# Differential attention: the six middle turns of the loop over batches written out on all five engines

## The reference, cut to what matters

```
x = x + layernorm(differential_attention(layernorm(x)))      # the stage of this case
x = x + layernorm(windowed_attention_and_gated_ffn(layernorm(x)))   # two layers
x = x + layernorm(diffusion_attention(layernorm(x)))
x = x + layernorm(expert_mixture(layernorm(x)))

# differential attention, for each batch and head, causal:
attn = softmax(Q1 K1^T / 4) - lam * softmax(Q2 K2^T / 4)
O = attn V;  O = O / rms(O) * rms_scale * 0.2;  out = concat(O) Wo^T
```

## Time and profile before

| | |
|---|---|
| median of 3 runs | 4381.61 us |
| the profiled execution's own time | 4382.84 us |
| its span, first to last instruction | 4381.0 us |
| the changed stage, up to the barrier | 1188 us |
| PE busy over the whole span | 3709.8 us (85%) |
| DVE, ACT, POOL busy | 2415.1, 1752.6, 1619.3 us |
| granted TensorE clock, mean | 0.924 |

### The profile page before, as it was taken

The page is one execution under the profiler, slowest core; times in us unless marked ns, Lnnn a source line. Parts: engine busy times, 40 slices in busy tenths (PEclk is TensorE's granted clock), DMA queues, the critical chain, the costliest instruction groups (busy, mean ns, idle before and its releaser), DMA issues. The chain is left out here.

```text
span 4381.0 us, 64166 instructions
## 1 busy us (share of the span) xinstructions
PE 3709.8 (85%) x17520; PEld 2209.8 (50%) x17584; DVE 2415.1 (55%) x6529; ACT 1752.6 (40%) x4010; POOL 1619.3 (37%) x1750
## 2 busy tenths in 40 slices
PE   6999999999689998997999899679999998459940
PEld 3555555566345555554555555335555554346630
DVE  6766676677465662224656433245566665345556
ACT  2544444455345554112555511035555545114420
POOL 2333333333466762004667512401222221352244
PEclk8999999999799999999999999879999999669975
DMA  6555665557201112443011211132222221249952
GB/s 103 71 74 68 84 84 79 71 65 92 67 25 39 48 43 99 158 164 105 34 38 48 74 46 60 41 79 53 61 56 54 54 50 47 89 166 312 312 169 70
DMA packets 230366, 378.28 MB, mean 86 GB/s; under 512 B 39822, under 2 KB 166099, under 8 KB 223699
## 3 DMA queue, kind: packets, MB, share of 16 engines
q1 hardware_dynamic: 216658, 355.13, 34.4%
q0 software_dynamic: 6144, 16.79, 1.2%
q10 hardware_dynamic: 7296, 3.22, 0.3%
HBM read 170.03 MB, written 84.93 MB: 58 GB/s over the span
## 5 line engine op out<-in xcount | busy, mean ns | idle before, releaser
L758 DVE CUSTOM_DVE_ANT_0 a_ps<-a_ps,a_mask 128x128 f32<-128x128 f32 (+3 forms) x1024 | 481.0, 513 | 219.1 <-PE a_ps L513 199.6
L2618 DVE TENSOR_REDUCE c_neg_max<-c_ps 128x1 f32<-128x512 f32 x512 | 340.8, 684 | 244.5 <-PE c_ps L2286 243.1
L2479 ACT ACTIVATE c_probsT<-c_ps 128x512 f32<-128x512 f32 x512 | 299.2, 598 | 400.1 <-PE c_ps L2298 391.2
L368 POOL TENSOR_SCALAR_AFFINE_SELECT a_probs_c<-a_probs_c 128x256 f32<-128x256 f32 (+1 forms) x384 | 185.8, 500 | 699.5 <-ACT a_probs_c L663 699.2
L663 ACT ACTIVATE a_probs_c<-a_ps 128x512 f32<-128x512 f32 x640 | 344.6, 603 | 119.5 <-PE a_ps L531 84.4
L513 PE MATMUL a_ps<-a_packed_qk 65*128 65x128 f32 (+3 forms) x1024 | 336.9, 373 | 53.5 <-DVE a_maxima L758 28.0
L1094 POOL TENSOR_TENSOR w_probs<-w_probs,w_inv 128x1024 f32<-128x1024 f32 x128 | 242.3, 1893 | 334.8 <-DVE w_inv L1457 334.8
L549 PE MATMUL a_ps<-a_probs_c,a_v 128*64 128x512 f32 (+3 forms) x2048 | 329.9, 468 | 1.8 <-POOL a_probs_c L368 0.8
L531 PE MATMUL a_ps<-a_packed_qk 67*128 67x512 f32 (+3 forms) x1024 | 288.8, 345 | 0.8 <-DMA a_packed_qk<-a_max_half 0.8
L2286 PE MATMUL c_ps<-c_packed_qk 68*128 68x512 f32 x512 | 263.2, 519 | 4.4 <-DVE c_neg_max L2618 2.2
L1349 ACT ACTIVATE w_probs<-w_ps_s,w_neg_max 128x256 f32<-128x256 f32 x512 | 236.0, 478 | 68.2 <-DVE w_neg_max L1452 66.9
(11 more groups left out here) (323 smaller groups left out, 7805.9 us busy)
## 6 DMA issues: line engine op xcount, KB each, us to landing
a_packed_qk<-a_halves SPq DMA_DIRECT2D x512, 128.0 KB, 4.6
d_w<-in_L_ffn_second SPq DMA_DIRECT2D x71, 516.0 KB, 5.0
d_w<-in_L_ffn_first SPq DMA_DIRECT2D x71, 512.0 KB, 5.1
rows_dram<-f_zeros SPq DMA_DIRECT2D x8, 4096.0 KB, 16.1
c_packed_qk<-c_halves SPq DMA_DIRECT2D x256, 128.0 KB, 2.4
w_v<-w_v_next SPq DMA_DIRECT2D x16, 1024.0 KB, 4.7
d_rows<-rows_dram SPq DMA_DIRECT2D x71, 128.0 KB, 4.3
mixed_dram<-d_y SPq DMA_DIRECT2D x71, 128.0 KB, 4.9
```

The lines of the kernel that those rows point to most:

```text
L758: last = nc.vector.tensor_tensor_reduce(tile, tile, mask[:, (NT - 1 - i) * P:], 1.0, -3e38, ALU.add, ALU.max, accum_out=maxima_of[:, hd // ...
L2479: nc.scalar.activation(probsT[:, q % 2, r, :], ps_again[u % 2][:, :], ACT.Exp).then_inc(exp_done.sem, 1)
L2618: nc.vector.tensor_reduce(neg_max[:, g % 2, 0, s % GS:s % GS + 1], bank("s", s)[:, :], AX.X, ALU.max, negate=True).then_inc(max_ready.sem, 1)
```

## The change: a Python loop in place of the hardware loop

```
@@ -264,7 +264,7 @@
             before()
             body(0, (0, 1))
-            with eng.Fori(1, B - 1) as b:
+            for b in range(1, B - 1):
                 body(b, (-1, 0, 1))
             body(B - 1, (-1, 0))
             drain(B)
```

## The result

The changed kernel takes 4353.17 us, the median of 5 runs (4336.20 to 4359.07), against 4381.61 of before (five runs beside it, 4377.87 to 4393.85): a ratio of 0.9924, with a 95% interval of 0.9902 to 0.9946. It is faster, by some 33 us by the ratio and 28 by the medians. The profiled execution took 4336.20 us, the fastest of the five.

A forecast was written before the change was run, and what follows sets the result against it. The prediction took instruction-fetch stalls on PE and DVE behind the loop's jump back as the bound at the seams: 24.5 us gained less 3 us of clock gives 21.5, so 4360 us at the median's level, range 4349 to 4372.

The forecast's parts named there:

- What bounds the seam: Between loop turns: PE and DVE wait for instruction fetch after the jump back; DVE idles 3.62 us.
- the register rows: In each turn, 266 rows on PE and the like elsewhere go; costed at nothing, as sequencers run ahead.
- the later loops keep their price: At L1022 and L2053, branches stay at some 0.2 us; the rival of lost place had 0.04.
- the straight code starves too: Rival, loop turns written out: late fetches still stall 3.62 us a turn; 4378 us, no change; chance 0.06.
- the branch costs only its own time: Rival, loop's jump back: five branches of about 108 ns, 0.5 us in all; 4381 us; chance 0.03.
- The seam, 5 x 4.89 = 24.5.: At five seams between turns: removing the taken branch gives back 4.89 us each, 24.5 us in all.
- the late transfer doesn't bite: Rival, at the seams: no 0.82 us wait for packed maxima, so 28.6 us gained; 4353 us; chance 0.13.
- the entry passage's 5.72: Seam from batch 0 into the loop, without a jump back: 22.69 us against 28.41, so 5.72 us given back.
- The clock near step 11, 3 us lost.: Mid-turn, turns 2 to 6: two of five get the long clock drop, losing 3 us.
- The bounds (7.9 gained to 7.7 lost): Near step 11, turns 2 to 6: extremes if all lose the clock drop or all get the long one.
- The upper end of the forecast's own range: Whole kernel: 4371 us, with the clock all lost and 3 us lost elsewhere.
- The term of 3 us for the rest of the program: Behind the first stage: clock drops may fall otherwise, worth 3 us either way.

The follow-up runs named there:

- e1: Kernel before, with two batches written in the loop's body, so it jumps back 2 times in place of 5; ratio 0.9968 to before.
- e2: Kernel before, with the loop made six loops of one turn each, keeping all register arithmetic but no jump back; ratio 0.9938 to before.
- e3: Kernel before, with only PE's six turns written out and the other engines keeping the loop; ratio 1.0019 to before.
- e4: Kernel before, with only DVE's six turns written out and the other engines keeping the loop; ratio 0.9972 to before.
- e8: Changed kernel, with the later loop at L1022 given three batches in its body, so it jumps back once in place of five times; ratio 0.9961 to before.
- e9: Changed kernel, with the later stages' loops (L1022, L1064, L2053, L2119) written out too; median 4345.83 us, ratio 0.9921 to before.
- e7: The changed kernel run again, nothing altered; ratio 0.9932 to before.
- e11: Changed kernel, with SP's normed store and residual load moved behind the packs of the next batch's heads 4 to 7; ratio 0.9940 to before.
- e12: The kernel before run again, nothing altered; median 4380.14 us of 10 runs, ratio 1.0004.

## Why the prediction was right and wrong

What bounds the seam was right: the sequencers wait for instructions behind the jump back, DVE is the later of the two that matter, and nothing else of the loop is seen to cost. e1 shows it by the number of jumps, e2 by keeping all but the jumps, e3 and e4 by engine, e8 by making a cheap loop dear, and the packets of code that start behind each dear branch and behind no cheap one. The changed kernel loads code as well, 118 such packets up to the second stage against 162 before, and doesn't rest for it. For the register rows no cost is seen (e2). That the later loops keep their price was right (the branch rows above, e9). The rivals "the straight code starves too" and "the branch costs only its own time" are refuted by the seams, where in the changed kernel PE has no rest over 0.5 us but that for the packed maxima.

The direction was right and the size short: I gave 21.5 us; the stage gave 33.2 in the first trace and 27.5 in the second (e7). The median, 4353.17, lies in the range of 4349 to 4372, but the time that follows from the ratio, 0.9924 of 4381.6, is 4348 and just under it. Over the five traces with everything written in the first stage and PE's order kept (the changed kernel, e7, e8, e9, e11) the second stage starts at 1157.4 us on average, against 1189.7 in the two of before: 32.3 us. Two terms of the sum were off.

*The seam, 5 x 4.89 = 24.5.* It was sized from one passage, the one into batch 7, and in that passage L531 waited 0.82 us for the packed maxima. I took this wait for a fixed follower of the stall's removal. That is the step that failed: the wait does come, but not at each seam and not at 0.82. In the changed kernel it is 0, 0, 0.18, 0 and 0.63 us at the five seams, in e7 0.37, 0, 0, 0 and 1.38. In the five traces it stands at 14 of 25 seams, with 0.10 to 1.38 us, and a seam is 22.7 us and this wait, 22.99 on average. So it was worth 0.3 us a seam. e12 has 0.78 at the same passage as before (23.49 us), so there it does recur, but the seams between turns don't follow it. Measured, the five seams of before take 142.1 us in all and those of the changed kernel 114.3, 27.8 us less, or 5.6 each; the average of the five traces is 27.5. That lies nearer to my rival of "the late transfer doesn't bite", 28.6 us, to which I gave 0.13, than to the 24.5, and I should have given it about as much as the forecast: both passages were one sample each, and the entry passage's 5.72 differed by just this wait.

*The clock near step 11, 3 us lost.* It gained 5.2 us: the six figures sum to 128.0 us before and 122.8 after, and 122.5 on average over the five traces against 127.2 over the two of before. Turns 2 to 6, which the term was for, gave 3.5 of the 5.2; turn 1, which I had left as it was, gave 1.7. The bounds (7.9 gained to 7.7 lost) held it, but my choice within them had the wrong sign. I took turn 1 and batch 7 as samples of what happens at any moment and gave no weight to batch 0, where the clock doesn't fall. Once the turns no longer last a steady 140 us, the figure goes through 19.3, 20.9 and 22.6, and most often it is below the 21.05 of before. Why the steady turn has the short drop in nine of the ten turns 2 to 6 of the two traces of before, rather than none, no run tells.

Both misses go the same way, and together, 27.8 + 5.2 = 33.0, they are nearly all of the stage's 33.2. The range had no room for them together: its low end, 4349, adds the gained clock to 24.5 alone. The rival's 28.6 with the same clock would have given 4381.6 - 28.6 - 7.9 = 4345. The upper end of the forecast's own range was off too: 24.5 less 7.7 and 3 leaves 13.8, so 4368 at the median's level and not 4371. The term of 3 us for the rest of the program was too small as well: the diffusion attention alone spreads over 15 us between traces of the same code.

## What to carry to other kernels

A long loop body is paid at each jump back, a short one isn't; look for the rest behind the branch on every engine, not for the branch's own time, since DVE's branch took 63 ns and cost more than PE's of 3454. Only the engines that have work ready at the seam and no room in the turn need to be written out: here two of five gave the whole gain. To size such a change, compare passages of the same work with and without the jump, take all of them with their spread, and count a wait seen once as a possibility, not as a term.

## What the runs showed of the hardware that I had not expected

Whether a jump stalls goes with the number of trace records in the body, by engine. ACT: 383 and 479 stall (2.4 to 4.6 us), 161 and 221 don't. PE: 1702 and 2177 stall (3.3 to 3.9 us), 723 and 1094 don't. DVE: 671 stall (3.4 to 5.1 us), 84, 225 and 248 don't. POOL: 184 and 242 don't. No run here lies between, so the edges are only bounded. Past the edge the length doesn't count: e1's bodies hold twice the records (3406 on PE), and its jumps cost PE 3.5 and 3.7 us. The kernel before loads code in each turn of L267, and none in a turn of L1022. Its transfers by queue and kind from 444 to 584, with packets, MB and the share of the engines' time:

```profile
q8 instruction: 9, 0.15, 0.4%
q14 instruction: 12, 0.10, 0.2%
```
